# Perceiver block on one core: the attention's value transfers go from ScalarE's queue to SP's, and the splitting of expert weights shifts by one block

## The reference

```
x = x + L0_xattn(layernorm(x), ctx_1024, ...)      # 3 iterations with a GRU
x = x + L0_attn(layernorm(x), Wqkv, bqkv, Wo, bo)
x = x + L0_ffn(layernorm(x), router_w, ...)

# attn, with H = 16 heads of hd = 32
qkv = (x @ Wqkv.T + bqkv).reshape(B, H, S, 3 * hd)
q, k, v = split(qkv, 3, axis=-1)
attn = softmax(einsum('bhsd,bhtd->bhst', q, k) / sqrt(hd), axis=-1)
vals = einsum('bhst,bhtd->bhsd', attn, v).reshape(B, S, D)
return vals @ Wo.T + bo

# ffn: E = 8 experts, the two best for each token, and 2 shared ones
expert(x) = (silu(x @ w1) * (x @ w3)) @ w2
```

## Time and profile before

| | |
|---|---|
| timed runs | 962.06, 965.24, 969.88 us; median 965.24 |
| profiled execution | 964.86 us, of which the span 963.1 us |
| TensorE busy | 786.8 us, 82% of the span |
| VectorE busy | 595.6 us, 62% |
| ScalarE busy | 367.1 us, 38% |
| head_attention | about 732.2 to 820.2 us in the span |

### The profile page before, as it was taken

The page is one execution under the profiler, slowest core; times in us unless marked ns, Lnnn a source line. Parts: engine busy times, 40 slices in busy tenths (PEclk is TensorE's granted clock), DMA queues, the critical chain, the costliest instruction groups (busy, mean ns, idle before and its releaser), DMA issues. The chain is left out here.

```text
span 963.1 us, 37792 instructions
## 1 busy us (share of the span) xinstructions
PE 786.8 (82%) x17278; PEld 658.6 (68%) x17278; DVE 595.6 (62%) x1119; ACT 367.1 (38%) x724; POOL 142.9 (15%) x390
## 2 busy tenths in 40 slices
PE   3697689989879989789979889775797876798990
PEld 1445679989879979779979889765555753543440
DVE  2777356876776957756947765423644677794222
ACT  3676415334425315434425411110255544362330
POOL 3020111211312121304021302010000000030003
PEclk9899889999999999999999999887696678798996
DMA  9867980263390390762470824103537500641525
GB/s 344 328 133 132 246 145 5 52 129 118 58 238 5 58 235 7 110 185 29 78 194 4 152 79 107 31 24 113 210 87 218 173 12 22 198 132 44 123 86 163
DMA packets 179530, 115.75 MB, mean 120 GB/s; under 512 B 145772, under 2 KB 158116, under 8 KB 176172
## 3 DMA queue, kind: packets, MB, share of 16 engines
q1 hardware_dynamic: 166624, 100.45, 41.2%
q10 hardware_dynamic: 11004, 7.61, 2.6%
q0 software_dynamic: 1744, 5.27, 1.9%
HBM read 61.94 MB, written 12.85 MB: 78 GB/s over the span
## 5 line engine op out<-in xcount | busy, mean ns | idle before, releaser
L988 PE MATMUL score<-qa,ctxT 128*128 128x64 f16 x3744 | 120.0, 195 | 22.5 <-issue 13.1
L988 PEld LDWEIGHTS score<-qa,ctxT 128*128 128x128 f16 x3744 | 116.1, 99 | 25.0 <-issue 14.5
L1007 PE MATMUL score<-qa,unit 128*128 128x64 f16 (+1 forms) x2496 | 122.4, 197 | 8.0 <-issue 6.2
L1007 PEld LDWEIGHTS score<-qa,unit 128*128 128x128 f16 (+1 forms) x2496 | 121.3, 101 | 11.1 <-issue 11.1
L1007 PE MATMUL score<-scratch,unit 128*128 128x64 f16 (+1 forms) x1248 | 120.8, 197 | 4.0 <-issue 4.0
L939 PEld LDWEIGHTS gate<-hs,whhT 128*128 128x128 f16 x3456 | 110.2, 99 | 16.2 <-issue 9.2
L939 PE MATMUL gate<-hs,whhT 128*128 128x64 f16 x3456 | 112.6, 195 | 9.2 <-issue 7.8
L1007 PEld LDWEIGHTS score<-scratch,unit 128*128 128x128 f16 (+1 forms) x1248 | 114.9, 101 | 1.9 <-issue 1.9
L939 PE MATMUL gate<-qa,Bt 128*128 128x64 f16 x3456 | 105.1, 193 | 3.7 <-DVE qa L762 2.8
L939 PEld LDWEIGHTS gate<-qa,Bt 128*128 128x128 f16 x3456 | 102.6, 98 | 4.1 <-DVE qa L762 3.0
L517 ACT ACTIVATE unit<-unit,rrow 128x512 f16<-128x512 f32 x96 | 65.4, 716 | 33.7 <-POOL rrow L96 18.3
(11 more groups left out here) (254 smaller groups left out, 1340.0 us busy)
## 6 DMA issues: line engine op xcount, KB each, us to landing
unit<-in_ctx_dram SPq DMA_DIRECT2D x23, 1024.0 KB, 9.8
wall<-in_L_ffn_routed_w_dram SPq DMA_DIRECT2D x24, 512.0 KB, 9.1
xg_scratch<-wall SPq DMA_DIRECT2D x1, 3840.0 KB, 15.1
y_scratch<-room ACTq DMA_DIRECT2D x15, 256.0 KB, 2.0
ctxT<-in_L_xattn_gru_wih_dram SPq DMA_DIRECT2D x3, 1024.0 KB, 17.5
ctxT<-in_L_xattn_gru_whh_dram SPq DMA_DIRECT2D x1, 3072.0 KB, 25.8
ctxT<-in_L_attn_Wqkv_dram SPq DMA_DIRECT2D x12, 256.0 KB, 6.9
ctxT<-in_L_ffn_shared_w_dram SPq DMA_DIRECT2D x6, 512.0 KB, 6.3
```

Source lines behind the costliest of these rows:

```text
L988: mm = pe.matmul(score[n][:, t * K:(t + 1) * K], a, q, start=(k == 0), stop=(k == 3 * DC - 1), skip_group_check=True)
L1007: mm = pe.matmul(score[n][:, dc * K:(dc + 1) * K], a, q, start=first, stop=True, skip_group_check=True)
```

## The change

SP's program now loads three experts, then does the four tiles' value transfers, each behind its wait for `vals_out`, and then loads the experts 3 and 4. ScalarE's program loses the transfers. The high halves of pieces 0 to 4 stay in the blocks 2 to 6; the low halves of pieces 0 to 4 move to the blocks 3 to 7, one block behind. Behind the last block two pieces (5 and 6) stand ahead of the last tile's halves in place of three (6 to 8), and nine stand behind in place of seven.

```
+AHEAD_IN = 3
...
         def _(sp):
             sp.dma_start(bo_row, dram.bo.partition_broadcast(P)).then_inc(bo_in, 16)
-            for n in range(EARLY):
+            for n in range(AHEAD_IN):
+                load_expert(sp, dram.routed, n, raw_of(e_all.wall, n), e_all.wall_in[n])
+            for t in range(RT):
+
+                sp.wait_ge(vals_out, 4 * (t + 1))
+                for ii in range(4):
+                    sp.dma_start(valsT[32 * ii:32 * ii + 32, :, t * P:(t + 1) * P],
+                                 vals[:, ii:HC:4, t * P:(t + 1) * P]).then_inc(moved[t], 16)
+            for n in range(AHEAD_IN, EARLY):
                 load_expert(sp, dram.routed, n, raw_of(e_all.wall, n), e_all.wall_in[n])
...
-            def vals_move(t):
-
-                act.wait_ge(vals_out, 4 * (t + 1))
-                for ii in range(4):
-                    act.dma_start(valsT[32 * ii:32 * ii + 32, :, t * P:(t + 1) * P],
-                                  vals[:, ii:HC:4, t * P:(t + 1) * P]).then_inc(moved[t], 16)
...
                 if k >= 3 and k % 2 == 1:
                     vals_high((k - 3) // 2)
-                if k >= 2 and k % 2 == 0:
-                    vals_move((k - 2) // 2)
-                if k >= 2:
+                if 2 <= k < B - 1:
                     wall_high(act, e_all, k - 2, k - 1)
-            vals_move(RT - 1)
-            wall_high(act, e_all, B - 2, B + 1)
+            wall_high(act, e_all, B - 3, B - 1)
             vals_high(RT - 1)
-            wall_high(act, e_all, B + 1, IN_HEADS)
+            wall_high(act, e_all, B - 1, IN_HEADS)
...
                 if k >= 5 and k % 2 == 1:
                     add_y((k - 5) // 2)
-                if k >= 2:
-                    wall_low(dve, e_all, k - 2, k - 1)
+                if k >= 3:
+                    wall_low(dve, e_all, k - 3, k - 2)
             values_out(B - 1)
             add_y(RT - 2)
-            wall_low(dve, e_all, B - 2, B + 1)
+            wall_low(dve, e_all, B - 3, B - 1)
             vals_low(RT - 1)
-            wall_low(dve, e_all, B + 1, IN_HEADS)
+            wall_low(dve, e_all, B - 1, IN_HEADS)
             add_y(RT - 1)
```

## The result

| | before | changed |
|---|---|---|
| median of 20 timed runs | 966.01 us | 963.31 us |
| range | 962.06 to 971.68 | 959.36 to 965.52 |
| ratio, 95% interval | | 0.9964, 0.9947 to 0.998 |
| profiled execution, its span | 963.1 | 961.9 |
| the stage of the attention, worked out below | 88.3 | 84.8 |

The changed kernel is faster by 0.36% (0.2 to 0.53), or 3.5 us of 966 by the ratio; the two medians lie 2.70 us apart. Against 961.3 forecast, 963.31 was measured. The forecast gain was 3.95. The profile is sharper, because in it the stage can be read by itself.

What follows compares the result with a forecast made beforehand. TensorE was busy 82% of the span; in block 2 VectorE's wait for ScalarE's split was wholly on the path. -2.9 - 0.85 + 0 - 0.8 + 0.6 = -3.95 from 965.24 gave 961.3 us, range 957.5 to 967.5.

Steps and rivals of the forecast that it cites:

- Term 1: Block 2: with the low half one block later, norm(3) starts at 758.65 in place of 761.57, -2.9 us.
- Term 2: Block 3: turn_probs(3) starts earlier, at the full clock, and takes 1.09 us for 1.97, -0.85 us.
- Term 3: Block 4: TensorE's own work is the path and project(0) hides the removed wait, 0 us.
- Term 4: Block 6: TensorE's 0.80 us wait for norm(7) goes, -0.8 us.
- Term 5: Tail: add_y(3) comes 11.3 us after values_out(7) against 10.7, with nine low halves behind, +0.6 us.
- SP's queue: Experts 3 and 4, loaded behind the transfers, are issued by 815.5, before the stage's end, so nobody waits; cost 0.
- A: Rival: only issue time goes, norm stays held by the split; -0.8 us, 964.4 us; chance 0.05.
- C: Rival: the low clock lasts through blocks 4 to 7, making it slower; +3.65 us net, 968.9 us; chance 0.08.
- B: Rival: clock not up in block 2, so Term 1 and Term 2 vanish; -0.2 us, 965.0 us; chance 0.27.
- D: Rival: clock stays up before turn_probs(4), speeding it, scores(6) and project(0); -7.45 us, 957.8 us; chance 0.07.
- E: Rival: loads of experts 3 and 4 hold the router's weights; at half the rate +4, 965.4 us; chance 0.03.

Runs made afterwards that it cites:

- e1: Kernel before with only the transfers moved to SP's queue, the splits in their old places; ratio 0.9981, 964.76 us.
- e2: Kernel before with only the splits reordered (low halves one block later, new tail order), transfers still on ScalarE; ratio 0.9941, 961.40 us.
- after_again: The changed kernel itself, measured a second time; ratio 0.9988 against the kernel before, 962.75 us.
- e6: Changed kernel with twelve matmuls, result never read, ahead of the stage's first scores; ratio 0.9972 against the kernel before, 962.93 us.
- e4: Changed kernel with all five experts loaded ahead of the transfers in SP's queue; ratio 0.9975 against the kernel before, 964.06 us.
- e2_again: Second measurement of e2, run beside the changed kernel; ratio 0.9961 against the kernel before, 962.00 us.
- e9_gap_before: Kernel before with six copies on VectorE ahead of norm(2), meant to lower TensorE's clock in block 2; ratio 1.0006, 964.95 us.

## Why the prediction was right, point by point

- **Term 1, block 2, -2.9: right.** norm(3) stands at 26.59 for 29.37, -2.8, with the exponentials as its releaser. e1 shows that moving the transfers alone gives 0.6 there; e2 shows that moving the low half alone gives all of it (norm(3) at 26.30 and 26.45), so the two parts overlap.
- **Term 2, the clock in block 3, -0.85: right.** 1.09 for 1.97 us, and norm(4) gained another 0.8. What the prediction does not say is that this 0.8 needs both halves of the change: in e2, with the issues still on ScalarE, turn_probs(3) took 1.09 as well, but norm(4) gained nothing beyond norm(3) (2.9 to 3.0 in all).
- **Term 3, block 4, 0: right.** norm(5) came 6.9 us earlier, and norm(6) only 3.6, as norm(4) had. TensorE's chain from norm(4) to norm(6) took 19.8 us on both sides; 0.6 less in turn_probs(4) and 0.5 more in project(0) cancelled. This pair moves from profile to profile (turn_probs(4) 1.38, 1.53, 1.09 beside project(0) 4.85, 4.70, 5.21 in changed, after_again and e6), so the exact 0 is partly luck. A VectorE wait of 3.29 us was removed for nothing.
- **Term 4, block 6, -0.8: right in kind, 0.2 too much.** turn_probs(7) has no wait any more, and values_out(7) gained 0.6 on norm(6): project(1) took 4.25 for 3.98, at the low clock for longer.
- **Term 5, the tail, +0.6: +0.74.** The step that was a little small is the landing: from values_out(7) to vals_high(3) 4.04 us and not 3.85. SP's four issues of this transfer took 2.52 us, 0.63 each, as ScalarE's four at the same place did before (2.55), and not the 0.59 of the other transfer on SP. Nine low halves took 6.24 us, as worked out (6.2).
- **SP's queue, 0: right**, by e4.
- **The sum**, 3.95 forecast, 3.49 in the stage, 0.36% of 966 = 3.5 in the times. The range, 957.5 to 967.5, was ten microseconds wide (3.8 were put below and 2.5 above for one scatter of about 3) and held no change as well. The time alone would hardly have shown the forecast wrong; what bears it out is the signs in the profile, which came term by term.
- **The rivals.** A (only the issue time) is refuted by e2, where the issues are still there and 3.4 of the stage's 3.5 us are gained (in `e2_again`; 1.2 in the profile with the long project(0)); e1, which has only the transfers' move, got about what A said, 1.1 in the stage. So the Trainium skill's rule on issuing engines ("DMA: Bandwidth & Descriptors", "Issuing engines are not separate DMA queues") holds for the half of the change that it speaks of, with 0.58 us at the place where it was the path; it says nothing on the half that paid. One issue is small beside its transfer here too, 0.63 us against 2.1 to landing, but four in a row took 2.5. C appeared in a small form. B and D were in no profile, and B's late clock could not be made. E is refuted.
- **What was off** was the weight: B had 0.27, for the reason that the clock came up in the first instruction of the block where the gain is. Twelve profiles of kernels whose TensorE work is alike up to there show it within half a microsecond of that instruction's start (turn_v(2) took 0.68 to 0.86), so it was no accident of one execution. The median's own scatter was judged rightly: one kernel gave 0.9964 and 0.9988.

## What to carry to other kernels

A wait on an engine is worth its length only while no other engine's chain is longer at that place: of three like stalls removed here, 3.3 to 4.4 us each, one gave 2.8, one nothing, one 0.6. What hides a stall can itself be a slow stretch: the stall that was worth nothing came out as soon as TensorE's block 4 ran at the full clock. When two engines hand one piece of work to each other, let the second take it one round later; and where an engine owes another one an instruction whose data are already there, put it ahead of the work that the other needs only later. That was worth more than twice the whole change in the stage, 1.6 of its 8.1 us by a better clock. Where the gain is smaller than the scatter of the times, measure the stage from its own first instruction in the profile.

## What the runs showed of the hardware

- A TensorE that is busy is not one whose clock is up. In the changed kernel, in the stage's first 23 us, it was busy for 20.04 with small float32 matmuls and stayed at 1.2 GHz throughout (columns: busy us of TensorE, its weight loads, VectorE, ScalarE and GpSimd, then granted clock, DMA share, GB/s):

```profile
734.00:757.00 23.00, 20.04 (x191) 17.36 (x192) 15.88 (x26) 14.06 (x18) 1.81 (x1) 0.50 0.67 221
```

- The copy from float32 to float16 within SBUF with one source took 0.35 us for 128 x 512 on VectorE, half of the 0.69 that the two-source operations of the same size took (`e9_gap_before`).
- The issue of a 64 KB transfer over 32 partitions took about 0.63 us on ScalarE and on SP alike where the engine did nothing else (2.55 and 2.52 for the four behind the last block); in block 2 the four on ScalarE took 2.93. There ScalarE issued the first at 757.33, while three instructions that stand ahead of it in its program started only behind that time (the exponentials at 757.98). It cost ScalarE only what was left over when they ended: 0.62 us in block 2, 1.02 in block 4, 2.22 in block 6.
- The twelve-matmul group of 128 x 512 took from 2.75 to 5.30 us in one and the same stage (the first profile of `e2_reorder_only`), by the clock it met. That, not the instructions, made the 2.2 us between two profiles of one kernel.
